# Layer 0 of batch 0 with 512-column products over all eight PSUM banks, and only its first weight block by halves

## What is computed

```python
# layer 0: x + x @ W0^T + b0 + (x @ sign) * coeff, sign = 2*mask - 1, one mask a batch
output = jnp.einsum('bsi,oi->bso', hidden_states, W) + b
sign = (2 * mask - 1).astype(hidden_states.dtype)
diff = jnp.einsum('bsi,bio->bso', hidden_states, sign)
return output + diff * coeff[:, None, None]
# layer 1: x + x @ W1^T + b1 + 2 * (x @ A) @ B, A and B chosen for each batch
base_out = jnp.einsum('bti,oi->bto', x, W) + b
lora_h = jnp.einsum('bti,bir->btr', x, A)
lora_out = jnp.einsum('btr,bro->bto', lora_h, Bm)
return base_out + lora_out * SCALING
```

## Time and profile before

| what | us |
|---|---|
| median of three executions | 392.39 |
| the profiled execution | 392.74 |
| its span, first to last instruction | 390.9 |
| TensorE busy | 382.0 (98%) |
| VectorE busy | 245.9 (63%) |
| ScalarE busy | 178.1 (46%) |
| GpSimd busy | 49.7 (13%) |

### The profile page before, as it was taken

How to read it: one execution, slowest core, us unless ns; L and a number is a source line. 1 busy time by engine, 2 the same in 40 slices (tenths; PEclk the granted TensorE clock), 3 DMA queues, 4 the chain that set the end, 5 groups by cost and what they waited for, 6 DMA issues and landing times.

```text
span 390.9 us, 5982 instructions
## 1 busy us (share of the span) xinstructions
PE 382.0 (98%) x2334; PEld 359.1 (92%) x2334; DVE 245.9 (63%) x299; ACT 178.1 (46%) x313; POOL 49.7 (13%) x44
## 2 busy tenths in 40 slices
PE   8879999999999999999999999999999999999997
PEld 8879998998989999989999899899998999998996
DVE  3978989997177932788437981579617794281200
ACT  3546946656155622556235651464515563252221
POOL 2235910020003000030000300012000300002000
DMA  8999817873544633544526436164253562001011
GB/s 288 409 397 364 305 48 223 293 219 108 195 115 161 190 81 135 162 147 157 171 60 196 150 104 216 59 215 140 65 202 111 167 186 106 6 2 54 2 54 55
DMA packets 28078, 61.76 MB, mean 158 GB/s; under 512 B 2554, under 2 KB 3730, under 8 KB 28050
## 3 DMA queue, kind: packets, MB, share of 16 engines
q1 hardware_dynamic: 25232, 52.70, 41.6%
q10 hardware_dynamic: 2754, 8.66, 5.6%
q0 software_dynamic: 64, 0.01, 0.0%
HBM read 52.97 MB, written 8.39 MB: 157 GB/s over the span
## 4 chain that ended last, share of the span: by engine, by line
PE 83%; DVE 6%; DMA 4%; issue 3%; ACT 2%; SPq 1%; ACTq 0%; DVEq 0%
PE z_ps L385 43%; PE y_ps L347 23%; PE y_ps L353 12%; DMA ring<-in_mask 4%; DVE ring L680 3%; PE y_ps L385 2%; PE z_ps L429 2%; DVE wc_lo L688 2%; ACT wc_hi L499 1%; PE y_ps L317 1%; PE y_ps L327 1%; DVE y_two L727 0%; PE t_ps L420 0%; DVE y_raw L721 0%; ACT z_rows L552 0%
## 5 line engine op out<-in xcount | busy, mean ns | idle before, releaser
L385 PE MATMUL z_ps<-w_hi,y_two 128*128 128x344 f32 (+1 forms) x736 | 184.0, 323 | 1.3 <-DVE y_two L727 0.7
L385 PEld LDWEIGHTS z_ps<-w_hi,y_two 128*128 128x128 f32 x736 | 129.5, 188 | 3.0 <-DVE y_two L727 1.0
L347 PE MATMUL y_ps<-x_two,wc_hi 128*128 128x512 f32 x448 | 127.5, 395 | 0.0
L688 DVE SCALAR_TENSOR_TENSOR wc_lo<-ring,coeff_neg,wc_hi 128x1024 fp32r<-128x1024 f32 (+1 forms) x67 | 92.5, 1381 | 47.3 <-ACT wc_hi L499 46.5
L385 PE MATMUL z_ps<-w_lo,y_two 128*128 128x344 f32 (+1 forms) x368 | 118.3, 321 | 0.0
L499 ACT ACTIVATE wc_hi<-ring,coeff_neg 128x1024 fp32r<-128x1024 f32 (+1 forms) x67 | 74.6, 1115 | 71.5 <-PE y_ps L353 37.3
L680 DVE SCALAR_TENSOR_TENSOR ring<-ring,coeff_two,w_t 128x1024 f32<-128x1024 int32 (+1 forms) x67 | 86.6, 1301 | 8.2 <-DMA ring<-in_mask 7.3
L347 PEld LDWEIGHTS y_ps<-x_two,wc_hi 128*128 128x128 f32 x448 | 78.1, 189 | 10.9
L353 PEld LDWEIGHTS y_ps<-x_two,wc_lo 128*128 128x128 f32 x448 | 70.9, 189 | 8.4
L353 PE MATMUL y_ps<-x_two,wc_lo 128*128 128x256 f32 x448 | 78.2, 281 | 0.0
L385 PEld LDWEIGHTS z_ps<-w_lo,y_two 128*128 128x128 f32 x368 | 69.3, 188 | 0.0
(11 more groups left out here) (49 smaller groups left out, 182.3 us busy)
## 6 DMA issues: line engine op xcount, KB each, us to landing
ring<-in_mask SPq DMA_DIRECT2D x63, 512.0 KB, 4.4
x_raw<-in_x SPq DMA_DIRECT2D x31, 256.0 KB, 6.3
out<-z_rows ACTq DMA_DIRECT2D x15, 512.0 KB, 3.2
w_raw<-in_w SPq DMA_DIRECT2D x8, 512.0 KB, 10.3
w_t<-in_w SPq DMA_DIRECT2D x7, 512.0 KB, 9.3
b_raw<-in_lora_b SPq DMA_DIRECT2D x8, 256.0 KB, 3.6
w_t<-in_w SPq DMA_DIRECT2D x2, 256.0 KB, 3.7
ring<-in_mask SPq DMA_DIRECT2D x2, 256.0 KB, 4.8
```

What stands on the lines that cost most here:

```text
L347: pe.matmul(y_ps[o % HT][:, 0:2 * T], w, x_two[:, k, :, :], start=(k == 0), stop=False, skip_group_check=True)
L385: ins = pe.matmul(z_bank(b, s, g)[:, 0:EDGES[g + 1] - EDGES[g]], ys[:, k, s * P:(s + 1) * P], w[:, k, EDGES[g]:EDGES[g + 1]], start=(k == ...
L688: dve.scalar_tensor_tensor(out=wc_lo[:, k % RING, lo:hi], in0=sums[:, mask_entry(b, k) % RING, lo:hi], scalar=coeff_neg[:, b:b + 1], in1=w ...
```

## The change

In batch 0 of layer 0 each of the eight output blocks gets a PSUM bank of its own: output blocks 0 to 7 lie in `z_ps0`, `z_ps1`, `z_ps2`, `y_ps0`, `y_ps1`, `y_ps2`, `y_ps3`, `t_ps`. Output blocks 0 and 1 (`EARLY`) are still made with two matmuls of 256 columns on one half of a bank, and read as before. The other six are made with one matmul of 512 columns and are then copied, summed, rounded and split as in the later batches. Layer 1 of batch 0 may write a bank only when that bank has been read. Its order of products is changed at the start: (0,0), (0,1), (0,2) for k = 0 and 1, then (1,0), then (1,1). `HALVED` is 1: blocks 1 and 2 of the weights are made whole. On VectorE `x_low(0, 2)` and `x_low(0, 3)` come later: behind the low weights of block 3 and of block 5.

```diff
-    HALVED = 3
+    HALVED = 1
...
-        def first_bank(o):
-
-
-            return t_ps[:, 0:T] if o == 1 else y_ps[o // PAIR][:, (o % PAIR) * T:(o % PAIR + 1) * T]
+
+
+        EARLY = 2
+
+        def y_bank(b, o):
+            if b > 0:
+                return y_ps[o % HT]
+            return (*z_ps, *y_ps, t_ps)[o]
+
+        def y_sums(b, o):
+
+            return KT * b + o + 1 - EARLY
+
+        def y_split(b, k):
+
+            return k + 1 if b == 0 and k < EARLY else XG * b + k // PAIR + EARLY
...
-                    ys = first_bank(o)
                     w = wc_hi[:, k % RING, o * P:(o + 1) * P]
-                    for n in range(2):
-                        pe.matmul(ys, w, x_two[:, k, n, :], start=(k == 0 and n == 0 and (o == 1 or o % PAIR == 0)),
-                                  stop=False, skip_group_check=True)
+                    if o < EARLY:
+                        for n in range(2):
+                            pe.matmul(y_bank(0, o)[:, 0:T], w, x_two[:, k, n, :], start=(k == 0 and n == 0),
+                                      stop=False, skip_group_check=True)
+                    else:
+                        pe.matmul(y_bank(0, o)[:, 0:2 * T], w, x_two[:, k, :, :], start=(k == 0), stop=False,
+                                  skip_group_check=True)
 
             def layer0_low(k):
 
                 for o in range(KT):
                     if o == 0 or (k < HALVED and o == HT):
                         pe.wait_ge(wc_lo_done, parts(0, k, o // HT))
-                    ys = first_bank(o)
                     w = wc_lo[:, k % RING, o * P:(o + 1) * P]
-                    ins = pe.matmul(ys, w, x_two[:, k, 0, :], start=False, stop=(k == KT - 1), skip_group_check=True)
-                    if k == KT - 1 and o % PAIR == PAIR - 1:
+                    ins = pe.matmul(y_bank(0, o)[:, 0:T], w, x_two[:, k, 0, :], start=False, stop=(k == KT - 1),
+                                    skip_group_check=True)
+                    if k == KT - 1:
                         ins.then_inc(y_full, 1)
...
-                    pe.wait_ge(y_lo_done, max(k + 1, PAIR * (g + 1) if s == 1 else 0))
+                    pe.wait_ge(y_lo_done, y_split(0, k))
+                    if k == 0:
+
+                        o = NG * s + g
+                        if o < EARLY:
+                            pe.wait_ge(y_lo_done, o + 1)
+                        else:
+                            pe.wait_ge(y_sum_done, y_sums(0, o))
...
-                    for s, g in ((0, 0), (0, 1), (0, 2), (1, 0)):
-                        first_products(s, g, [k])
+                    for g in range(NG):
+                        first_products(0, g, [k])
+                first_products(1, 0, range(PAIR))
...
+            def y_high_early(o):
+
+                act.wait_ge(y_full, o + 1)
+                act.activation(y_two[:, 0, o, :], y_bank(0, o)[:, 0:T], ACT.Identity,
+                               bias=b0_cols[:, o:o + 1]).then_inc(y_hi_done, 1)
...
-            for g in range(XG):
-                y_high_first(g)
-                w1_high(g + 1)
-            for k in range(XG + 1, KT):
+            w1_high(1)
+            y_high_early(0)
+            y_high_early(1)
+            y_copy(0, 2)
+            y_copy(0, 3)
+            w1_high(2)
+            y_high(0, 1)
+            y_copy(0, 4)
+            w1_high(3)
+            y_copy(0, 5)
+            y_high(0, 2)
+            w1_high(4)
+            y_copy(0, 6)
+            y_copy(0, 7)
+            y_high(0, 3)
+            for k in range(5, KT):
...
-            weights_sum(0, 1, 0)
-            weights_sum(0, 1, 1)
+            weights_sum(0, 1)
             x_low(0, 1)
-            weights_low(0, 1, 0)
-            weights_sum(0, 2, 0)
-            weights_low(0, 1, 1)
-            weights_sum(0, 2, 1)
-            weights_low(0, 2, 0)
+            weights_low(0, 1)
+            weights_sum(0, 2)
             weights_sum(0, 3)
-            weights_low(0, 2, 1)
-            x_low(0, 2)
-            for k in range(HALVED, KT):
+            weights_low(0, 2)
+            for k in range(3, KT):
                 step(0, k)
-                if k == HT:
-                    x_low(0, 3)
+                if k in (3, 5):
+                    x_low(0, (k + 1) // PAIR)
             w1_low(0)
+            w1_low(1)
             dve.wait_ge(cols_in, 16)
-            y_low_first(0)
-            w1_low(1)
-            y_low_first(1)
+            y_low_early(0)
+            y_low_early(1)
+            y_sum(0, 2)
+            y_sum(0, 3)
             w1_low(2)
+            y_low(0, 1)
+            y_sum(0, 4)
             w1_low(3)
-            y_low_first(2)
+            y_sum(0, 5)
+            y_low(0, 2)
             w1_low(4)
-            y_low_first(3)
-            for k in range(XG + 1, KT):
+            y_sum(0, 6)
+            y_sum(0, 7)
+            y_low(0, 3)
+            for k in range(5, KT):
```

46 lines of the change are left out of this document (18 added, 28 removed).

## The result

The changed kernel takes 393.31 us in the median of 22 executions (392.11 to 394.98), the kernel before 392.19 us on the same chips (22 executions, 391.74 to 393.19). The forecast was 393.1 us. The medians lie 1.1 us apart, the forecast said 0.7.

The account below looks back on a forecast made before the run. VectorE's queue was taken to bound up to 90.01 us: 2.6 us late at `x_low(1, 0)`, 1.1 at `x_low(1, 1)`, 0.7 left after the waits. Added to the median 392.39 that gives 393.1 us, range 392.0 to 394.2.

Parts of the forecast that it names:

- What bounds: VectorE's queue ends last from 53.59 to 90.01 us; TensorE then waits 0.7 us for y's low part in batch 1.
- TensorE's gain: Layer 0 of batch 0: 48 wide matmuls save 0.007 us each, 0.35 us in all, which comes to nothing.
- Rival C: TensorE's gain counts: last block of layer 0 ends earlier, y chain starts earlier, 392.3 to 392.7 us; chance 0.03.
- Way of y: Splitting y on VectorE and ScalarE: 1.56 us more VectorE work plus waits for ScalarE; `x_low(1, 0)` 2.6 us late.
- What stays: VectorE, `x_low(1, 0)` to 90.01 us: GpSimd's 2.1 us paid again, `x_low(1, 1)` 1.1 us late, 0.7 us left.
- Rival A: Delay absorbed: batch 1's sum not held by GpSimd again, VectorE up to 2.1 us earlier, 392.2 to 392.5; chance 0.15.
- Blocks made whole: Weight blocks 1 and 2 of batch 0: put at 0, between a gain of 0.1 and a loss of 0.2 us.
- x_low: End of layer 0: `x_low(0, 3)` ahead of block 7's sum delays it 0.1 us, up to 0.35 if GpSimd holds it.
- Part 1 of w1 ahead of the first y: VectorE before layer 1: w1 parts 0 and 1 at 33.5 and 34.9, early part at 36.0 us; nothing charged.
- Rival B: Slower engine handovers or GpSimd meetings make TensorE wait in layer 1 of batch 0: 393.5 to 394.4 us; chance 0.27.
- The wait at the transposes: TensorE loses some 0.3 us, as ScalarE makes batch 1's weights ahead of `h_copy`; none of it reaches the end.
- Rival D: Whole blocks let mask 6 land up to 0.7 us sooner, moving layer 0 and y: 391.7 to 392.3 us; chance 0.10.

Follow-up runs that it names:

- e3b: The kernel before with three unused subtractions of 1024 columns on VectorE ahead of `x_low(1, 0)`, 3.4 us more in its queue: 393.41 us, 1.35 over before.
- e5: The kernel before with lora B's low part made on VectorE instead of GpSimd: 391.20 us, 1.01 below before, ratio 0.9975.
- e4: The changed kernel with lora B's low part made on VectorE instead of GpSimd: 391.58 us, 0.63 below before, ratio 0.9986.
- e7: The changed kernel run again unedited, for another profiled execution and its spread: 393.07 us, 0.94 over before, ratio 1.0035.
- e8: The kernel before with weight blocks 1 and 2 made whole, `x_low` left where it was: 392.22 us, 0.01 over before, ratio 1.0001.
- e2: The kernel before with weight blocks 1 and 2 made whole and `x_low` moved as in the change: 392.64 us, 0.58 over before, ratio 1.0017.

## Why the prediction was right, and where it missed

- **The number.** 393.1 us was forecast and 393.31 measured, but 0.2 us of that closeness is luck: the forecast was added to a median of three, 392.39, and the median of 22 is 392.19. In the difference, 0.7 was forecast and 1.1 measured.
- **What bounds.** Right. TensorE does wait at 90 us for the low part of y, 0.85 us now; after it, the time is the same (390.8 - 89.92 = 300.9 us, as in the earlier trace rows). e3b and e5 show VectorE's queue as the bound from both sides.
- **TensorE's gain, 0.35 us, hidden.** Right: the six wide matmuls take 32.55 to 33.94, 0.23 us each, as the row of before said; e4 against e5 shows no gain even where VectorE has room. Rival C is out. The rule of the Trainium skill (TensorE: Matmul & The Clock Gate, section Back-to-back issue gap), some 131 ns for each matmul of 512 columns in a stream, does not hold for this kernel's matmuls.
- **Way of y.** `x_low(1, 0)` was walked to 15.4 us after block 7's low products; measured 15.64. ScalarE's two stands were forecast to end at 41.7 and 45.4, from low products at 35.0; with low products at 33.94 they ended at 40.73 and 44.55, which is 6.79 and 10.61 us behind these, where 6.7 and 10.4 were said. Two of the walk's prices are a little off their rows: two low pairs take 1.35 us, some 0.65 each and not 0.60, and a sum takes some 0.33 from start to start and not 0.36; over three low pairs and six sums that cancels.
- **What stays.** The GpSimd instruction was paid again, as said, though on `x_low(1, 0)` (2.88 us) rather than on the sum behind it. `x_low(1, 1)` came 18.1 us after the first product, 18.0 forecast; the waits for h and at 58.8 went; 0.70 us were left at 58.70, 0.70 at 89.92 and 0.69 at the end, where the forecast has 0.6 behind the first product (59.5 - 36.7 against 58.79 - 36.61) and 0.1 ahead of it. e7's profile shows 0.4. Rival A is out.
- **Blocks made whole: 0, and x_low: 0.1 us.** The first is right (e8, +0.01). The second is the term of the sum that was mis-sized: from sum to sum it is 0.45 us in the changed kernel and 0.37 in e2, where I took 0.10 and named 0.35 as the bound, and e2 is 0.58 us over its before, e8 0.01. `x_low(0, 3)` itself takes 0.26 us longer in e2, the low part ahead of it 0.2 us longer in the changed kernel; that GpSimd's diagonal holds them is argued from the rows alone.
- **Part 1 of w1 ahead of the first y.** I had it end just as the first y was due and charged nothing. In the profile VectorE goes from the w1 parts to the early low part at 35.09 without a pause, 0.36 us after ScalarE was done with the high part, and the first product comes 35.82 - 33.94 = 1.88 us after the low products, not 1.71. That is 0.2 us in this profile, and between -0.1 and 0.3 in the others with part 1 in front. With the 0.3 us by which x_low was priced too low it would more than make up the 0.4 us between forecast and result; how much is the longer executions instead is open.
- **Rival B** did not happen in the profiled executions: TensorE doesn't wait inside layer 1 of batch 0. The wait at the transposes, 0.40 us, belongs to the forecast itself, which had 0.3, and it has no effect on the end. But six of the changed kernel's 22 executions lie in B's 393.5 to 394.4 us, and none of them was profiled; B stays a possible account of these.
- **Rival D** is out: e8's whole blocks bring nothing. By the forecast's own signs it would have been C or D, since `x_low(1, 1)` started at 53.91, before 54, and the first product at 35.82, before 36.3. Both are times from the start of the span, and they lie in the scatter of the front that kernels with an unchanged front show too. Those signs were badly chosen; counted from the first product they would have held.
